# A third staging buffer for keys and queries, and a new place for the FFN input's conversions

## What is computed

```
for each sequence x (1024 x 256):
    y = layernorm(x)
    Q, K, V = y @ w_qkv                       (Q / 4), 16 heads
    Ql, Kl = means of Q, K over groups of 16 tokens (64 landmarks)
    k1 = softmax(Q Kl^T); k2 = softmax(Ql Kl^T); k3 = softmax(Ql K^T)
    att = (k1 inverse(k2)) (k3 V) @ w_proj    inverse: 6 iterations
    x = x + layernorm(att)
    y = layernorm(x)
    base = y @ W_base + b_base
    for e in 0..7: h = relu(y Wd1[e] + bd1[e]); loss[e] = mean((h Wd2[e] + bd2[e] - y)^2)
    e = argmin(loss)
    x = x + layernorm(base + relu(y Wa_down[e] + ba_down[e]) Wa_up[e] + ba_up[e])
```

## Time and profile before

| what | value |
|---|---|
| median of 3 runs | 2231.13 us (2229.5 to 2233.48) |
| the profiled execution | 2235.6 us |
| its span (first to last instruction) | 2233.9 us |
| PE busy | 2022.2 us, 91% |
| DVE, ACT, POOL busy | 1442.4, 864.7, 700.7 us |
| mean granted clock of PE | 0.971 |
| DMA queue share of the 16 engines | 28.1% |

### The profile page before, as it was taken

One profiled execution on the slowest core, in us unless ns is written; L12 is line 12 of the kernel. 1 busy time (PEld: TensorE's weight loads), 2 busy tenths in 40 slices (PEclk: granted clock), 3 DMA queues, 4 the chain that ended last, 5 costly groups with the idle time before them and its releaser, 6 DMA issues.

```text
span 2233.9 us, 59429 instructions
## 1 busy us (share of the span) xinstructions
PE 2022.2 (91%) x25341; PEld 1314.7 (59%) x25341; DVE 1442.4 (65%) x3303; ACT 864.7 (39%) x1509; POOL 700.7 (31%) x918
## 2 busy tenths in 40 slices
PE   4889999999999999999999998999999999999955
PEld 2655757566574756657475564757657475665724
DVE  4667575776757676675766767576675757767541
ACT  3344344343434434343344434334343443434320
POOL 4152142422315232332523223252231524223052
PEclk9999999999999999999999999999999999999977
DMA  6213151331414123152422315132231513313020
GB/s 156 49 53 70 30 131 33 88 64 31 115 30 125 39 79 66 20 134 30 117 47 71 67 28 133 31 103 51 67 78 31 129 34 86 68 36 91 12 57 19
DMA packets 232974, 150.74 MB, mean 67 GB/s; under 512 B 153035, under 2 KB 203732, under 8 KB 232693
## 3 DMA queue, kind: packets, MB, share of 16 engines
q1 hardware_dynamic: 232710, 146.95, 28.1%
HBM read 36.98 MB, written 16.78 MB: 24 GB/s over the span
## 4 chain that ended last, share of the span: by engine, by line
PE 57%; DVE 20%; SPq 8%; issue 5%; ACT 4%; POOL 3%; DMA 2%; DVEq 1%; POOLq 0%; ACTq 0%
PE NS L991 11%; PE ringF L1199 11%; SPq L432 8%; PE ringA L1158 5%; PE ringF L1184 5%; PE ringA L885 4%; DVE mx L1560 3%; PE ringF L1232 3%; DVE mx L1546 3%; DVE stage L1634 3%; PE KV L1072 2%; PE ringF L885 2%; PE ringA L1058 2%; PE ringA L1034 2%; PE ringF L1234 2%
## 5 line engine op out<-in xcount | busy, mean ns | idle before, releaser
L1199 PE MATMUL ringF<-x,H 128*128 128x256 f16 x1536 | 237.9, 273 | 0.0
L1560 DVE TENSOR_REDUCE mx<-ringA 128x8 f32<-128x512 f32 x256 | 175.4, 686 | 91.0 <-PE ringA L1034 89.9
L687 ACT ACTIVATE E<-ringA,score_scale 128x512 f32<-128x512 f32 x256 | 175.5, 686 | 132.7 <-PE ringA L1058 132.6
L1199 PE MATMUL ringF<-H 128*128 128x128 f16 x1024 | 204.4, 220 | 1.4 <-DVE H L1645 1.4
L521 POOL TENSOR_SCALAR vtmp<-mv,eps_ffn 128x8 f32<-128x8 f32 x16 | 5.1, 316 | 606.6 <-DVE mv L1391 606.6
L1611 DVE SCALAR_TENSOR_TENSOR X<-X,NS 128x320 f32<-128x320 f32 x160 | 78.0, 488 | 179.1 <-PE NS L991 173.9
L885 PE MATMUL ringA<-xT,wqkv 128*128 128x512 f16 x768 | 176.5, 379 | 17.8 <-ACT QS L705 11.7
L1184 PE MATMUL ringF<-wd,x2T 128*128 128x512 f16 x768 | 185.4, 380 | 3.4 <-DVE H L1645 3.2
L695 ACT ACTIVATE E<-ringA,score_scale 128x512 f32<-128x512 f32 x256 | 158.6, 685 | 73.4 <-PE ringA L1089 73.4
L1546 DVE TENSOR_REDUCE mx<-ringA 128x1 f32<-128x512 f32 x256 | 160.1, 682 | 30.1 <-PE ringA L1025 30.1
L521 POOL TENSOR_SCALAR vtmp<-mv,eps_ln 128x8 f32<-128x8 f32 x32 | 9.9, 310 | 506.1 <-DVE mv L1391 506.1
(11 more groups left out here) (262 smaller groups left out, 4277.1 us busy)
## 6 DMA issues: line engine op xcount, KB each, us to landing
KS<-stage SPq DMA_DIRECT2D x384, 64.0 KB, 2.0
QS<-stage SPq DMA_DIRECT2D x384, 64.0 KB, 2.0
xin<-in_L_attn_x_dram SPq DMA_DIRECT2D x16, 1024.0 KB, 10.9
xres<-in_L_attn_x_dram SPq DMA_DIRECT2D x16, 1024.0 KB, 8.0
out_dram<-yout SPq DMA_DIRECT2D x16, 1024.0 KB, 5.5
QS<-LB SPq DMA_DIRECT2D x16, 512.0 KB, 4.4
E<-in_L_attn_w_qkv_dram SPq DMA_DIRECT2D x1, 768.0 KB, 7.0
H<-in_L_ffn_Wd_dram SPq DMA_DIRECT2D x2, 256.0 KB
```

The lines of the kernel that those rows point to most:

```text
L687: A(E[:, k % ESLOTS, :], ps[:, :], ACT.Exp, scale=score_scale[:, 0:1]).then_inc(freed["s3"].sem, 1)
L1199: ins = MM(dst, H[:, a, t, own], src, start=first and i == 0, stop=last and i >= 3, skip_group_check=True)
L1560: V_.reduce_max(mx1[:, t, 8 * h:8 * h + 8], take(b, "m1", k)[:, :].rearrange("p (a m) -> p a m", a=8), AX.X)\
```

## The change

`stage` gets a third slot. The groups 0, 1, 2, 3 use the slots 0, 1, 2, 0. ACT waits for DMAs only before group 3, and there for those of group 0. On ACT the groups 2 and 3 stand in a row, and both conversions of the FFN input follow. Of the eight constant products before m3 5 two are left. `svT` stays in the slots 0 and 1.

```
-        stage = sb("stage", [P, 2, 2, N], F16)
-        svT = stage[:, :, :, :].rearrange(...)
+        stage = sb("stage", [P, 3, 2, N], F16)
+        STAGE_OF = (0, 1, 2, 0)
+        svT = stage[:, 0:2, :, :].rearrange(...)
...
-                                         stage[32 * q:32 * q + 32, j % 2, part, :]).then_inc(stk[j].sem, 16)
+                                         stage[32 * q:32 * q + 32, STAGE_OF[j], part, :]).then_inc(stk[j].sem, 16)
...
             def staged(b, js):
                 for j in js:
-                    if j >= 2:
-                        act.wait_ge(stk[j - 2].sem, stk[j - 2].at(b, 12))
+                    if j == 3:
+                        act.wait_ge(stk[0].sem, stk[0].at(b, 12))
...
-                staged(b, (2,))
+                staged(b, (2, 3))
                 if ffn:
-                    halves2(b - 1, (0,))
-                staged(b, (3,))
-                if ffn:
-                    halves2(b - 1, (1,))
+                    halves2(b - 1, (0, 1))
                 values(b, (2, 3))
...
                     if k == 5:
-                        keep_warm(512, 8)
+                        keep_warm(512, 2)
```

More of the change, by code:

```diff
@@ L115, in sandwich_kernel @@
         xlT = sb("xlT", [P, 2, KC, M], F16)
-        stage = sb("stage", [P, 2, 2, N], F16)
-        svT = stage[:, :, :, :].rearrange("p a b n -> p (a b n)").bitcast(F32).rearrange("p (k n) -> p k n", k=KC)
+        stage = sb("stage", [P, 3, 2, N], F16)
+        STAGE_OF = (0, 1, 2, 0)
+        svT = stage[:, 0:2, :, :].rearrange("p a b n -> p (a b n)").bitcast(F32).rearrange("p (k n) -> p k n", k=KC)
         QS = sb("QS", [P, PAIRS, N], F16)
@@ L634, in staged @@
                 for j in js:
-                    if j >= 2:
-                        act.wait_ge(stk[j - 2].sem, stk[j - 2].at(b, 12))
+                    if j == 3:
+                        act.wait_ge(stk[0].sem, stk[0].at(b, 12))
                     for h in range(2):
                         k = 2 * j + h
-                        A(stage[:, j % 2, 0, h * HALF:(h + 1) * HALF], take(b, "pk", k)[:, :], ACT.Copy)\
+                        A(stage[:, STAGE_OF[j], 0, h * HALF:(h + 1) * HALF], take(b, "pk", k)[:, :], ACT.Copy)\
                             .then_inc(pk_hi.sem, 1)
@@ L1494, in staged @@
                     cols = slice(h * HALF, (h + 1) * HALF)
-                    V_.tensor_tensor(stage[:, j % 2, 1, cols], bank("pk", k)[:, :], stage[:, j % 2, 0, cols],
+                    V_.tensor_tensor(stage[:, STAGE_OF[j], 1, cols], bank("pk", k)[:, :], stage[:, STAGE_OF[j], 0, cols],
                                      ALU.subtract).then_inc(freed["pk"].sem, 1)
```

## The result

| | before | after |
|---|---|---|
| median of the runs taken side by side, us | 2232.31 (2229.5 to 2235.63, 4 runs) | 2195.66 (2192.99 to 2199.66, 4 runs) |
| ratio, 95% interval | | 0.984 [0.982, 0.9859] |
| profiled execution: time / span / mean granted clock | 2235.6 / 2233.9 / 0.971 | 2199.66 / 2197.9 / 0.976 |

The account below looks back on a forecast made before the run. PE was taken to wait for ACT's late copies of pk 6 and 7, with SP's queue a second chain about 0.9 us ahead of PE. 2231.1 - 21.5 (batches 1 to 15) - 1.9 (batch 0) = 2207.7 us, range 2196 to 2223.

Parts of the forecast that it names:

- The shift of the maxima: DVE, ahead of the loop: with pk 7 copied at once, the maxima start 1.87 us earlier.
- Two constant products for eight: PE before m3 5: removed six are worth nothing by themselves; left in, they cost 0.2 to 0.4 of 1.87 us.
- The conversions behind group 3 and the late wait for group 1: ACT: moving both costs 0 a batch; at most some 0.3 us of SP's transposes at risk.
- The gate: Loop start: s3 0 can't start before 2.15 us behind L408's issue on SP's queue; m1 2 follows 4.12 behind it.
- the first term: Batches 1 to 15: m1 2 behind L408 goes from 5.55 to 4.12 us, 1.43 a batch, 21.5 in all.
- the queue doesn't bind: Rival: group 2's and the fold rows' DMAs land early enough, all 1.87 us a batch arrives, 2201 us; chance 0.08.
- The new hole before m1 0 and s3 0: PE waits after hidden 3 for m1 0 and s3 0: about 0.8 us in the mean batch, up to 1.2 to 1.3.
- the slower rival: New idle time before s3 0, filler gone, brings clock falls of 2.0 us in each of 15 batches: 2248 us; chance 0.06.
- Batch 0: No FFN input there, L408 not held by SP's queue: the whole shift arrives, 1.9 us.
- The clock taken unchanged: Whole batches: number of clock falls, nine of 2.0 us, taken unchanged; between none and all worth -18 to +10 us.
- The rival of fewer falls: Whole batches: 0 to 4 clock falls in place of 9, 2190 to 2200 us; chance 0.12.
- The sign that I gave for it: Profile after: a mean clock leaving 0.971 by more than 0.01 would show that the clock had its say.

Follow-up runs that it names:

- The order alone: Kernel before with only ACT's new order (groups 2 and 3 in a row, conversions behind), two slots, eight constant products: 2233.59 us, ratio 1.0002.
- The extra issue: One unread 8 KB DMA added on SP ahead of the fold rows' DMA: 2235.37 us on the kernel before, 2195.67 on the changed kernel.
- the repeat above: Second measurement of the changed kernel with five constant products put into the 1.23 us hole ahead of s3 10: 2184.09 us, ratio 0.978.
- the slot alone: Kernel before with only the third slot and its waits, old order on ACT, eight constant products: 2218.15 us, ratio 0.9942.

## Why the prediction was right, and where it was short

**The shift of the maxima: right.** 1.87 us was forecast. Batch 13 shows 1.95, the mean 2.12 (18.48 to 16.36; batch 10 of before, with its fall, adds to it), and m1 0 came 1.84 us earlier in the mean (32.09 to 30.25).

**Two constant products for eight: right that taking them out pays in the new order, with the price mis-sized.** I put leaving them in at 0.2 to 0.4 us of the shift. The maxima come 0.66 us later with eight: m3 5 has to be made before DVE can start, about 0.4 us that the working left out. Of that 0.31 us reaches m1 0 and 0.19 m1 2. And "worth nothing by themselves, since PE waited behind them" was wrong for the old order. There they cut a hole of up to 3.00 us, and without them the kernel is 8.5 us slower. Here the page cited in the prediction was the better guide (the Trainium skill, TensorE: Matmul & The Clock Gate, section A second HAM failure mode: psum-queue depth-cycling): it tells of short idles between groups of products that made the clock go back and forth, and I had drawn from it that the filler has a use. The rows of the old order agree, with idle times of 1.75 to 3.00 us and six falls behind them. In the new order that idle time is gone, and the filler no longer has this use.

**The conversions behind group 3 and the late wait for group 1: right, at 0.** The transposes moved by 0.07 us a batch. The order alone shows that this hangs on the third slot: without it they move by 1.44.

**The gate: the mechanism was right, and the first term was short.** s3 0 comes 2.23 us behind L409 in the mean (2.15 forecast), m1 2 4.25 (4.12). The extra issue shows that the queue binds in after and didn't in before. But the sum took L408's issue as fixed, and that is the step that failed. It stands 9.15 us behind the transposes, not 9.64, and 0.42 us earlier from the batch's start, 6.3 us in all; m1 2 at 4.25 behind it and not 4.12 takes 2.0 of them back, nearly all of it by the late landing in batch 3. 1.43 + 0.42 - 0.13 = 1.72 us a batch. Nearly the whole shift of 1.87 arrived (1.71), so by size the rival "the queue doesn't bind" was nearer, though by mechanism it was wrong. Why the queue became shorter is only partly seen. Of the 0.49 us in the mean, 0.16 are a wait that went: in before the fold rows' DMA waited for `F3T` itself in the batches 10 (1.9 us) and 12 (0.4), and in after never. Another 0.17 is in the issue of the two transposes (4.87 to 4.70 us) and 0.16 in the last six DMAs of group 2 (4.42 to 4.26, while the first six take 3.7 in both). In seven of before's batches one of these six issues took 1.2 to 1.8 us for 0.59, and in three of after's. What holds them up stays open. Batch 13, with 4.99 and 4.05 us for the six, shows more than the mean. I should have asked why six equal issues took 4.99 us beside the 3.68 of the first six: a stretch longer than its twin is not a constant.

**What is late next: not seen.** After the change four chains meet within a few tenths of a us, in most batches: the transpose's landing with `hidden` 0 to 3 and then m1 0, the landing of group 2, the fold rows' DMA, and DVE's maxima for s3 1. Taking the fold rows' DMA out of them gives nothing, as the kernel with it on POOL shows.

**The new hole before m1 0 and s3 0: too large.** About 0.8 us was forecast. It is 0.56 in the mean, 0.46 without batch 3, and 0.23 in batch 13. Part of the idle time stands before `hidden` 0 instead, which waits for its transpose in most batches (0.14 us in the mean). No fall of the clock came behind it in after, so the slower rival, 2248, didn't come true. It wasn't groundless: behind the wait of 1.75 us before `hidden` 0, in batch 4 of the repeat above, the clock did fall.

**Batch 0: right.** 2.0 us for 1.9.

**The clock taken unchanged: wrong by about 8 us.** Nine falls (and one at a batch's head) became five. The rival of fewer falls, 2190 to 2200, has the measured time in its range and 2.0 us a fall about right, though it wanted no more than four falls; it came on top of the forecast. The sign that I gave for it, a mean clock more than 0.01 from 0.971, was too coarse: 0.976 was worth 8 us. With the hole filled in both kernels, the change is worth 25.1 us by the spans and 28.8 by the medians, and the forecast was 23.4. So the 12 us by which the forecast is off are two thirds clock, which nothing in the working would have given, and one third the queue. That the time came no further out than the low end is owed to the falls that this end allowed for. Why fewer falls come in after isn't shown. The hole of 1.23 us is in fourteen batches of each, and where it is filled no fall comes behind it. It is needed and doesn't decide alone, as the prediction had it, so a number of falls for a new kernel can't be forecast from these traces. But the hole was in the trace of before, and filling it there brings 17.9 us by the medians, nearly half of what the whole change brings.

## What to carry to other kernels

When a change moves a wait, look for every chain that ends within a us of it, and ask of each whether its length is fixed: a queue's stretch that is longer than its twin isn't a constant. Slots and order belong together; here the slot alone gave 0.47 us a batch, the order alone 0.12, and both 1.71. Price a constant product by the hole that it fills and by what waits behind it, not by its busy time, and compare kernels batch by batch at the same clock, since a median can hide a loss of 0.5 us a batch behind four falls fewer.

## What the runs showed of the hardware

- A hole of 1.23 us in an otherwise busy loop is followed by half clock, beginning 0.7 to 2.2 us behind its end, in some batches (five of fourteen in after, nine in before) and not in others. A whole batch with such a fall is 2.0 to 2.3 us longer. Five products of 512 columns in the hole left none in the two profiled executions.
- The spread of the kernel before from run to run goes with the clock: of 25 runs the fastest took 2220.23 us at a mean granted clock of 0.977, the slowest 2244.88 at 0.964.
- The usual 2.0 to 2.1 us to landing doesn't always hold: one DMA of 32 KB in after landed 3.9 us behind its issue. Of the DMAs of 64 KB issued by POOL the median was 2.2 us in batch 0 without transposes and 4.7 over all batches, where SP's took 2.1; the transposes beside them took 7.1 for 4.6.
